# Second attention: contexts, masks and ternary weights in smaller pieces, batch by batch, ternary weights last

## The reference, cut to what matters

```python
x = x + tanh(g_xattn[0]) * L0_xattn(layernorm(x), ctx, ...)
x = x + tanh(g_ffn[0]) * L0_ffn(layernorm(x), ...)            # 16 experts
x = x + tanh(g_xattn[1]) * L1_xattn(layernorm(x), ctx, mask, Wq, Wk, Wv, Wo)
x = x + tanh(g_ffn[1]) * L1_ffn(layernorm(x), W_up, W_gate, W_down)

# L1_xattn: x (4, 256, 256), ctx (4, 1601, 128), 16 heads of 128, 8 key heads
q = x @ Wq; k = ctx @ Wk; v = ctx @ Wv
scores = where(mask, q @ k.T / sqrt(128), -inf)
out = (softmax(scores) @ v) @ Wo

# L1_ffn, each of its three weights (262144 numbers) first:
scale = mean(abs(w)) + 1e-8
w = clip(round(w / scale), -1, 1) * scale
```

## Time and profile before

| | us |
|---|---|
| median of 3 runs | 1677.91 |
| lowest, highest | 1677.08, 1680.65 |
| the profiled execution | 1681.94 |
| its span, first to last instruction | 1680.6 |
| TensorE busy in it | 1460.4 |
| VectorE busy | 1244.0 |
| ScalarE busy | 1101.0 |
| GpSimd busy | 794.4 |

### The profile page before, as it was taken

The page is one execution under the profiler, slowest core; times in us unless marked ns, Lnnn a source line. Parts: engine busy times, 40 slices in busy tenths (PEclk is TensorE's granted clock), DMA queues, the critical chain, the costliest instruction groups (busy, mean ns, idle before and its releaser), DMA issues.

```text
span 1680.6 us, 25444 instructions
## 1 busy us (share of the span) xinstructions
PE 1460.4 (87%) x8460; PEld 711.5 (42%) x8460; DVE 1244.0 (74%) x2229; ACT 1101.0 (66%) x1996; POOL 794.4 (47%) x618
## 2 busy tenths in 40 slices
PE   5688887888878797788898989899899999999979
PEld 3243343343333343344444444344544455455445
DVE  6767667667786256478887768899589997788937
ACT  3556656756754755477786668678477775788724
POOL 3014013013130001077766749787486876577823
PEclk8798998998989999799999999999999999999989
DMA  4001200300340100100001000000000000000000
GB/s 154 1 1 29 52 2 2 60 1 2 60 176 1 51 1 5 40 20 6 1 1 32 29 21 6 26 1 1 5 26 1 26 1 1 1 1 1 1 0 26
DMA packets 20489, 36.70 MB, mean 22 GB/s; under 512 B 4898, under 2 KB 15238, under 8 KB 19334
## 3 DMA queue, kind: packets, MB, share of 16 engines
q1 hardware_dynamic: 20358, 35.07, 7.2%
HBM read 26.53 MB, written 1.15 MB: 16 GB/s over the span
## 4 chain that ended last, share of the span: by engine, by line
PE 35%; POOL 9%; issue 7%; DVE 5%; ACT 3%; POOLq 0%; DMA 0%; ACTq 0%; DVEq 0%; SPq 0%
PE BK L599 35%; POOL arena L1929 6%; DVE arena L1559 2%; DVE arena L1542 1%; ACT arena L1806 1%; ACT arena L1814 1%; POOL arena L1926 1%; POOL arena L1904 1%; ACT arena L1799 1%; POOL arena L1935 1%; POOL arena L1914 1%; DVE arena L926 0%; PE BK L906 0%; ACT L1799 0%; DVE arena L1573 0%
## 5 line engine op out<-in xcount | busy, mean ns | idle before, releaser
L599 PE MATMUL BK<-arena 128*128 128x512 bf16 (+14 forms) x8130 | 1414.1, 375 | 188.8 <-DVE arena L1380 43.4
L599 PEld LDWEIGHTS BK<-arena 128*128 128x128 bf16 (+7 forms) x8130 | 674.2, 115 | 897.7 <-issue 218.5
L1929 POOL TENSOR_TENSOR arena<-arena 128x512 f32<-128x512 f32 (+1 forms) x352 | 509.1, 1446 | 178.7 <-ACT arena L1799 154.6
L1559 DVE TENSOR_TENSOR arena<-arena 128x512 bf16<-128x512 f32 (+1 forms) x416 | 513.9, 1244 | 39.8 <-ACT arena L1806 39.1
L1799 ACT ACTIVATE arena<-BK,arena 128x512 f32<-128x512 f32 (+1 forms) x416 | 285.9, 687 | 131.7 <-PE BK L599 116.1
L1707 ACT ACTIVATE arena<-BK 128x512 f32<-128x512 f32 (+1 forms) x416 | 227.2, 604 | 95.0 <-PE BK L599 89.6
L1380 DVE TENSOR_REDUCE arena<-BK 128x1 f32<-128x512 f32 x384 | 244.2, 682 | 53.1 <-PE BK L599 52.2
L1806 ACT CAST arena<-arena 128x512 bf16<-128x512 f32 (+1 forms) x416 | 253.3, 609 | 0.0
L1814 ACT ACTIVATE arena<-BK 128x512 bf16<-128x512 f32 (+1 forms) x256 | 130.0, 508 | 87.7 <-PE BK L599 87.6
L1542 DVE CUSTOM_DVE_ANT_0 arena<-BK,arena 128x512 bf16<-128x512 f32 (+1 forms) x256 | 145.5, 568 | 47.4 <-PE BK L599 41.8
L1848 POOL TENSOR_TENSOR arena<-arena 128x256 f32<-128x256 f32 (+6 forms) x45 | 30.2, 671 | 184.1 <-ACT arena L1646 181.7
(11 more groups left out here) (175 smaller groups left out, 850.1 us busy)
## 6 DMA issues: line engine op xcount, KB each, us to landing
arena<-arena SPq DMA_DIRECT2D x144, 50.0 KB, 2.2
arena<-in_ctxT SPq DMA_DIRECT2D x8, 800.5 KB, 4.4
arena<-in_ctxk SPq DMA_DIRECT2D x4, 768.0 KB
arena<-in_wo SPq DMA_DIRECT2D x1, 2048.0 KB, 7.5
arena<-in_wqT SPq DMA_DIRECT2D x1, 2048.0 KB, 7.8
arena<-in_x SPq DMA_DIRECT2D x4, 256.0 KB, 9.4
arena<-in_rsel SPq DMA_DIRECT2D x1, 1024.0 KB, 9.1
arena<-in_rw1T SPq DMA_DIRECT2D x1, 1024.0 KB, 5.0
```

Of the source, the lines that this page charges most:

```text
L599: return T.matmul(out_, lhsT, rhs, start=start, stop=stop, skip_group_check=True)
L1559: V.tensor_tensor(Pl[k][0:m, :], P1[k][0:m, :], Ph[k][0:m, :], ALU.subtract).then_inc(p_low, 1)
L1929: G.tensor_tensor(acc[0:m, g % 2, :], acc[0:m, g % 2, :], P1[k][0:m, :], ALU.add).then_inc(summed1, 1)
```

## The change

- Background steps are at kt 1, 3, 6, 9 and 11.
- A context is cast in two halves (`cx`), differenced in two (`cz`, a piece of its own), and split in two (`cy`), each in its own step; GpSimd's low part of the difference is four instructions in two steps. After `cxl` one more step is left empty.
- A mask is seven pieces: two halves of the product, two of the sum, L928 with five small operations, two halves of the result. GpSimd's copy and difference are two of each, in the step of the last.
- GpSimd's ternary difference (L1940) is two instructions within its step.
- Order: context 1, values 1, mask 1, norm (2,2); at tile 104 or later norm (2,3), context 2, values 2, mask 2; at tile 208 or later context 3, values 3, mask 3, then the three ternary weights.
- Batch 0's pieces in stage 1 are spread over eight steps, where they had six.
- Semaphore counts and waits follow.

```diff
         def context():
-            piece("cx", 0)
-            yield
-            yield
-            piece("cy", 0)
+            piece("cx", 0, 0)
+            piece("cx", 0, 1)
+            yield
+            piece("cz", 0, 0)
+            yield
+            piece("cz", 0, 1)
+            piece("cy", 0, 0)
             piece("mbl")
             yield
-            for k in range(3):
-                piece("mk", 0, k)
-                yield
+            piece("cy", 0, 1)
+            piece("mk", 0, 0)
+            yield
+            piece("mk", 0, 1)
+            piece("mk", 0, 2)
+            yield
+            piece("mk", 0, 3)
+            piece("mk", 0, 4)
+            yield
+            piece("mk", 0, 5)
+            yield
+            piece("mk", 0, 6)
+            yield
...
             assert ("m1n", 8 * b) not in self.slot
-            for k in range(3):
+            for k in range(7):
                 piece("mk", b, k)
                 yield
 
         def context(b):
             piece("cxl", b)
             yield
-            piece("cx", b)
-            yield
-            piece("cy", b)
-            yield
+            yield
+            for kind in ("cx", "cz", "cy"):
+                for half in range(2):
+                    piece(kind, b, half)
+                    yield
...
             pass
-        bg = chain(context(1), values(1), masked(1), self.norm(to, 2, 2), self.norm(to, 2, 3), context(2), values(2),
-                   context(3), values(3), masked(2), ternary(0), masked(3), ternary(1, 2))
+        now = [0]
+
+        def later(tile):
+            while now[0] < tile:
+                yield
+
+        bg = chain(context(1), values(1), masked(1), self.norm(to, 2, 2),
+                   later(104), self.norm(to, 2, 3), context(2), values(2), masked(2),
+                   later(208), context(3), values(3), masked(3), ternary(0, 1, 2))
...
             g, kt = s // NKT, s % NKT
+            now[0] = s
...
                 next(og, None)
-            if kt % 4 == 1:
+            if kt in (1, 3, 6, 9, 11):
...
             kept, off = mask_temp(b)
-            if k == 0:
-                dve.wait_ge(ld_row, 16 * (b + 1))
-                dve.wait_ge(*emptied("fold", H - 1))
-                dve.wait_ge(ct_high, b + 1)
-                dve.wait_ge(mx_ready, b)
-                if b:
-                    dve.wait_ge(ct_done, 4 if b == 1 else 2 * B)
-                V.tensor_tensor_reduce(out=kept, in0=cth[:, b, :], in1=mb8[:, :], scale=1.0, scalar=0.0, op0=ALU.mult,
-                                       op1=ALU.add, accum_out=mst[:, 0:1]).then_inc(dve_chain.sem, dve_chain.up())
-                V.tensor_reduce(mst[:, 1:2], mb8[:, :], AX.X, ALU.add).then_inc(dve_chain.sem, dve_chain.up())
-            elif k == 1:
+            own = ((0, HALF), (HALF, S2))
+            if k < 2:
+                w_ = slice(*own[k])
+                if k == 0:
+                    dve.wait_ge(ld_row, 16 * (b + 1))
+                    dve.wait_ge(*emptied("fold", H - 1))
+                    dve.wait_ge(ct_high, 2 * b + 2)
+                    dve.wait_ge(mx_ready, b)
+                    if b:
+                        dve.wait_ge(ct_done, 2 * b + 2)
+                V.tensor_tensor_reduce(out=kept[:, w_], in0=cth[:, b, w_], in1=mb8[:, w_], scale=1.0, scalar=0.0,
+                                       op0=ALU.mult, op1=ALU.add,
+                                       accum_out=mst[:, k:k + 1]).then_inc(dve_chain.sem, dve_chain.up())
+            elif k < 4:
+                V.tensor_reduce(mst[:, k:k + 1], mb8[:, slice(*own[k - 2])], AX.X,
+                                ALU.add).then_inc(dve_chain.sem, dve_chain.up())
+            elif k == 4:
                 V.tensor_scalar(off, mb8[:, :], 1.0, None, ALU.subtract).then_inc(mask_done, 1)
                 dve.wait_ge(dve_chain.sem, dve_chain.n)
-                V.tensor_scalar(mst[:, 2:3], mst[:, 1:2], 1.0, None, ALU.max).then_inc(dve_chain.sem, dve_chain.up())
+                V.tensor_tensor(mst[:, 4:6], mst[:, 0:4:2], mst[:, 1:4:2], ALU.add).then_inc(dve_chain.sem, dve_chain.up())
                 dve.wait_ge(dve_chain.sem, dve_chain.n)
-                V.reciprocal(mst[:, 3:4], mst[:, 2:3]).then_inc(dve_chain.sem, dve_chain.up())
+                V.tensor_scalar(mst[:, 6:7], mst[:, 5:6], 1.0, None, ALU.max).then_inc(dve_chain.sem, dve_chain.up())
                 dve.wait_ge(dve_chain.sem, dve_chain.n)
-                V.scalar_tensor_tensor(out=mst[:, 4:5], in0=mst[:, 0:1], scalar=-1.0, in1=mst[:, 3:4], op0=ALU.mult,
+                V.reciprocal(mst[:, 7:8], mst[:, 6:7]).then_inc(dve_chain.sem, dve_chain.up())
+                dve.wait_ge(dve_chain.sem, dve_chain.n)
+                V.scalar_tensor_tensor(out=mst[:, 0:1], in0=mst[:, 4:5], scalar=-1.0, in1=mst[:, 7:8], op0=ALU.mult,
                                        op1=ALU.mult).then_inc(dve_chain.sem, dve_chain.up())
             else:
+                w_ = slice(*own[k - 5])
                 dve.wait_ge(dve_chain.sem, dve_chain.n)
                 dve.wait_ge(mask_done, b + 1)
-                V.scalar_tensor_tensor(out=kept, in0=off, scalar=mst[:, 4:5], in1=kept, op0=ALU.mult,
-                                       op1=ALU.add).then_inc(mk_done, 1)
+                t = V.scalar_tensor_tensor(out=kept[:, w_], in0=off[:, w_], scalar=mst[:, 0:1], in1=kept[:, w_],
+                                           op0=ALU.mult, op1=ALU.add)
+                if k == 6:
+                    t.then_inc(mk_done, 1)
 
         def pool_mask(b, k):
-            if k == 2:
+            if k == 6:
                 kept, _ = mask_temp(b)
                 pool.wait_ge(mk_done, b + 1)
                 if b >= 2:
                     pool.wait_ge(*filled("mb", 8 * (b - 1) - 1, 3, 1))
-                G.tensor_copy(cmb[:, b % 2, :], kept[:, S2 - HALF:S2])
-                G.tensor_tensor(cmd[:, b % 2, :], kept[:, 0:HALF], kept[:, S2 - HALF:S2], ALU.subtract).then_inc(mx_ready, 1)
+                for lo, hi in ((0, 401), (401, HALF)):
+                    G.tensor_copy(cmb[:, b % 2, lo:hi], kept[:, S2 - HALF + lo:S2 - HALF + hi])
+                    t = G.tensor_tensor(cmd[:, b % 2, lo:hi], kept[:, lo:hi], kept[:, S2 - HALF + lo:S2 - HALF + hi],
+                                        ALU.subtract)
+                t.then_inc(mx_ready, 1)
...
                                            in1=x_sb[:, tk, :], op0=ALU.mult, op1=ALU.add).then_inc(free[i], 1)
-                elif kind == "cx":
-                    b, = arg
-                    dve.wait_ge(ct_high, b + 1)
+                elif kind == "cz":
+                    b, half = arg
+                    lo, hi = ((0, 673), (673, S2 - 256))[half]
+                    dve.wait_ge(ct_high, 2 * b + 2)
                     dve.wait_ge(ct_done, 2 * b + 1)
-                    V.tensor_tensor(ctf[b][:, 0:S2 - 256], ctf[b][:, 256:S2], ctf[b][:, 0:S2 - 256],
+                    V.tensor_tensor(ctf[b][:, lo:hi], ctf[b][:, 256 + lo:256 + hi], ctf[b][:, lo:hi],
...
                 elif kind == "cx":
-                    b, = arg
+                    b, half = arg
+                    w_ = (slice(0, HALF), slice(HALF, S2))[half]
                     act.wait_ge(ld_ctf[b], 16)
                     act.wait_ge(p_used, 208)
-                    A.copy(cth[:, b, :], ctf[b]).then_inc(ct_high, 1)
+                    A.copy(cth[:, b, w_], ctf[b][:, w_]).then_inc(ct_high, 1)
                 elif kind == "cy":
-                    b, = arg
-                    act.wait_ge(ct_step, b + 1)
+                    b, half = arg
+                    w_ = (slice(0, 673), slice(673, S2 - 256))[half]
+                    act.wait_ge(ct_step, 2 * b + half + 1)
                     act.wait_ge(*filled("fold", H - 1))
-                    A.copy(dch[b][:, :], ctf[b][:, 0:S2 - 256]).then_inc(ct_step_high, 1)
+                    A.copy(dch[b][:, w_], ctf[b][:, w_]).then_inc(ct_step_high, 1)
...
                     G.tensor_tensor(hsh[:, ch, :], hsh[:, ch, :], sr[:, :], ALU.mult).then_inc(hs_done, 1)
-                elif kind == "cx":
-                    b, = arg
-                    pool.wait_ge(ct_high, b + 1)
+                elif kind == "cx" and arg[1]:
+                    b = arg[0]
+                    pool.wait_ge(ct_high, 2 * b + 1)
                     pool.wait_ge(*filled("fold", H - 1))
                     G.tensor_tensor(ctl[:, b, 0:256], ctf[b][:, 0:256], cth[:, b, 0:256], ALU.subtract).then_inc(ct_done, 1)
                 elif kind == "cy":
-                    b, = arg
-                    pool.wait_ge(ct_step_high, b + 1)
-                    for lo, hi in ((0, 448), (448, 896), (896, S2 - 256)):
+                    b, half = arg
+                    pool.wait_ge(ct_step_high, 2 * b + half + 1)
+                    for lo, hi in (((0, 337), (337, 673)), ((673, 1009), (1009, S2 - 256)))[half]:
```

(13 more changed lines are left out.)

## The result

The changed kernel takes **1670.37 us** (median of 20 runs, 1665.71 to 1682.05) against 1677.89 for the kernel before in the same runs: a ratio of 0.9961, interval [0.9948, 0.9975]. It is 7 us faster; 25 were forecast (1653, range 1632 to 1672), and rival 2 had 1669.

What follows compares the result with a forecast made beforehand. TensorE's own work sets a 24.23 us pass floor; contexts and masks cost 50.5 us above it. Terms -26 + 1 + 2 - 2 = -25 took the profiled 1681.9 to 1656.9, less 4.0 for the median: 1653 us, range 1632 to 1672.

Steps and rivals of the forecast that it cites:

- rival 2: Stage 2: halves at kt 9, 11 and 1 add up as one block for lack of VectorE room; 1669 us, 17%.
- Sign and floor: Whole kernel: faster with chance 0.84; TensorE's own work keeps a quiet pass of stage 2 at 24.23 us.
- Contexts and masks in pieces: Stage 2 background: smaller pieces cut the cost from 50.5 us to 8 a batch, 24 for three; -26.
- one slope: VectorE blocks in stage 2: free up to about 0.7 us, above it about 2.2 us lost for each us.
- the step of 2 us: Mask step of L928 with four small operations: priced at 1.0 us, where the slope gave 2.9.
- rival 4: Stage 2: VectorE pieces start behind GpSimd's lock and carry 0.73 us more each; +10, 1688 us, 10%.
- Ternary last: Ternary pieces at the end, 33 steps over passes 20 to 26: +2 us (-2 to +7).
- Partly hidden beside the projection of pass 24: Ternary pieces in pass 24: part of their cost hidden beside the output projection; counted within +2.
- Order and gates: Batches 2 and 3 held back in stage 2, nobody waits; norm (2,3) moves into pass 8: +1 (0 to 2).
- Stage 1: Context 0 in stage 1, around which TensorE idles 7.2 us: -2, bounds -6 and +3.
- Sum: Whole kernel: -26 + 1 + 2 - 2 = -25 us, giving 1653 us.

Runs made afterwards that it cites:

- e8: Changed kernel with background steps at kt 1, 3, 6 and 9 only, none at kt 11: 1661.82 us, 0.9904 of the kernel before.
- e12: Kernel of e11 with the masks back in the kernel before's three VectorE pieces: 1671.70 us, 0.9945 of the kernel before.
- e1: Changed kernel with the background step at kt 3 moved to kt 5: 1671.30 us, 0.9952 of the kernel before.
- e2: Changed kernel with the same halves not spread: a mask's pieces in three steps, a context's in two, other steps empty: 1704.14 us.
- e4: Changed kernel with GpSimd's running sum over 8 of 512 columns, the rest left out: 1610.14 us.
- e9: Kernel before with GpSimd's running sum over 8 of 512 columns, the rest left out: 1622.37 us.
- e7: Changed kernel with the background at kt 1, 5 and 9 from tile 260 on: 1671.73 us.
- e10: Kernel of e8 with GpSimd's ternary difference over 8 of 512 columns, the rest set to zero once: 1664.15 us.
- e11: Kernel of e8 with the second ternary comparison and GpSimd's difference never before kt 5: 1653.32 us, 0.9842 of the kernel before.
- e3: Kernel before, whole pieces at kt 1, 5 and 9, with only the change's order and two gates: 1679.42 us, 1.0005.
- e5: Changed kernel with the masks in the kernel before's three VectorE pieces, in the same spread slots: 1676.56 us.

## Why the forecast was wrong

- **Sign and floor: right.** The quiet pass stayed, the pieces were what cost.
- **Step that failed: "Contexts and masks in pieces", -26, measured -18.** Of its 8 us a batch 5.7 were the mask's and 2.3 the context's, so 17 and 7 for three. The masks took 22, the contexts 10.3. I priced a piece by its length alone, by one slope. The three blocks above 0.7 us that gave it all stood at kt 9, or ran on behind it (L924, L1523 and L1603), and I used it for every slot but that of the step of 2 us, for which pass 12 already showed a lower price at kt 1. The runs show that the slot decides: in e8 the products are longer and the masks cost 10.3 in place of 22. Beside that the lengths were off. I had at most 1.27 us for a half of the product and 0.94 for a half of the result, and batch 1's took 1.70, 0.99, 1.96 and 1.05.
- Rival 2 came nearest. It said that VectorE has no room between kt 9, 11 and the next 1; I gave it 17% and argued against it with TensorE's idle 5.2 us in pass 2. That was misread: TensorE's idle time there was the loss, not room of VectorE. The right row was VectorE's 27.24 busy of 32.0 us. That the halves cost more with steps at kt 9 and 11 is shown (e8); that they add up there as one block is not (e8, e12). Its 1669 lies near the 1670 measured partly by luck: it had 3 us for ternary and norm, which took 6, and left the masks at 26, which took 22.
- **The contexts' 3 us too much are GpSimd's.** Pass 10 loses 3.2 us behind kt 7, with the low parts (L1943) at kt 2 and 5, and e1, which moves them, brings the pass from 3.7 to 1.0. I had counted GpSimd's context pieces with the values at 1.1 a batch.
- **VectorE's wait for GpSimd was at work, without reaching rival 4's size.** Halves that are not spread cost 5 us a mask more than the whole pieces (e2), and beside full sums the change brings 12 us of the 23 that it would bring beside narrow ones (e4, e9).
- **"Ternary last", +2, measured +6.** I charged VectorE's waits and cost GpSimd's pieces at nothing beyond them. The missing term is the queue of GpSimd: difference, two running sums, diagonal, TensorE. It shows for twe at kt 1 to 3 (e7, e10, e11). The order alone has the smaller part: in e3 the ternary pieces cost 12 us. The row stood in the kernel before too, in pass 7, with a context's low parts ahead of the diagonal:
```profile
931.50 0.69 DVE L1542 CUSTOM_DVE_ANT_0 arena<-BK,arena 128x512 bf16<-128x512 f32 x1 [4.01 <-PE BK L599]
```
"Partly hidden beside the projection of pass 24" was the reverse, 5.1 us more there.
- **Order and gates, +1: right.** Norm (2,3) adds 3.5 us to pass 8 and takes as much out of passes 3 to 5; e3 has 1.0005.
- **Stage 1, -2: wrong sign, +1.3.** Expert steps 18 to 28 take 37.2 in place of 35.9 us, in every kernel with this plan. Which piece does it, no run here took apart; with whole masks there (e5, e12) it is 38.2. And steps 28 to 31, 5.1 us before and in the profile after, take 7.5 or 7.6 in five and 6.7 in two of the other eight traces with this plan. No trace shows which of these the 20 runs had.
- **Sum.** -18 + 0 + 6 + 1.3 = -10.7, the profiles have -10.8, and the medians -7.5. The 3 us between the last two stay open: the start of stage 2 scatters by more than that, and the 1.6 to 2.5 us of stage 1 just named could be part of them.
- The range held the time, at its upper edge, because it was drawn to just past rival 2, and not by the bounds of the terms.
